# Feature products in quarters of the array and earlier in each block, and a subtraction in four parts, in a recommender kernel

## The reference

```python
e = emb_tables[jnp.arange(F)[None, :], x]             # B=1024, F=32, D=64
gram = jnp.einsum('bid,bjd->bij', e, e)
cross = gram[:, iu, ju]                               # the 496 pairs i < j
h = jnp.concatenate([e.reshape(B, F * D), cross], axis=1)
h = jax.nn.relu(h @ W1 + b1)                          # 2544 -> 1024
h = jax.nn.relu(h @ W2 + b2)                          # 1024 -> 512
y = jax.nn.sigmoid(h @ W3 + b3)                       # 512 -> 1000
```

## Time and profile before

| | |
|---|---|
| median of 3 runs | 507.16 us (505.77 to 508.83) |
| profiled execution | 505.47 us, span 503.7 us |
| TensorE matmul busy | 403.9 us (80%) |
| VectorE, ScalarE busy | 241.4 us (48%), 214.4 us (43%) |
| GpSimd busy | 334.9 us (66%) |
| mean granted TensorE clock | 0.922 of full |
| DMA | 80.15 MB, mean 159 GB/s |

### The profile page before, as it was taken

One profiled execution on the slowest core, in us unless ns is written; L12 is line 12 of the kernel. 1 busy time (PEld: TensorE's weight loads), 2 busy tenths in 40 slices (PEclk: granted clock), 3 DMA queues, 4 the chain that ended last, 5 costly groups with the idle time before them and its releaser, 6 DMA issues.

```text
span 503.7 us, 8367 instructions
## 1 busy us (share of the span) xinstructions
PE 403.9 (80%) x3328; PEld 395.1 (78%) x3328; DVE 241.4 (48%) x326; ACT 214.4 (43%) x358; POOL 334.9 (66%) x517
## 2 busy tenths in 40 slices
PE   0066766767769999878699999968899999897895
PEld 0066766766779999868599999958899999797895
DVE  2233333332348665444348664633586666444650
ACT  3122222223146555543247446442475556434642
POOL 6887888888888878877878778778788880000000
PEclk9997787786979999998889999989799999998998
DMA  7423343321754766623856667618658666167412
GB/s 234 108 62 107 106 105 103 105 65 25 230 189 144 228 188 203 209 64 124 271 191 180 207 197 216 196 23 270 207 164 271 184 181 218 44 216 259 139 51 81
DMA packets 32600, 80.15 MB, mean 159 GB/s; under 512 B 6802, under 2 KB 13106, under 8 KB 32050
## 3 DMA queue, kind: packets, MB, share of 16 engines
q1 hardware_dynamic: 24370, 71.22, 44.8%
q0 software_dynamic: 8192, 8.40, 7.3%
HBM read 69.22 MB, written 10.39 MB: 158 GB/s over the span
## 4 chain that ended last, share of the span: by engine, by line
PE 43%; POOL 33%; issue 10%; DMA 5%; DVE 4%; ACT 2%; SPq 1%; another core or an unknown queue 1%; ACTq 0%; DVEq 0%; POOLq 0%
POOL emb L278 27%; PE h1p L455 8%; PE h1p L456 8%; PE h1p L457 8%; POOL gap L284 6%; PE misc L455 4%; PE misc L485 4%; PE misc L457 4%; PE misc L456 4%; DVE dg L401 3%; DMA gc<-gram_scratch 2%; PE misc L470 2%; ACT dg L315 1%; DMA emb<-tables_dram,idx 1%; DMA gram_scratch<-dg 1%
## 5 line engine op out<-in xcount | busy, mean ns | idle before, releaser
L278 POOL DMA_INDIRECT emb<-tables_dram,idx x256 | 277.0, 1082 | 77.2 <-POOL gap L284 40.6
L385 DVE TENSOR_TENSOR wlo<-wraw,whi 128x1024 fp32r<-128x1024 f32 (+1 forms) x112 | 134.8, 1221 | 63.2 <-ACT whi L301 52.7
L455 PE MATMUL h1p<-xhi,whi 128*128 128x256 f32 x512 | 154.7, 302 | 1.0 <-issue 1.0
L301 ACT CAST whi<-wraw 128x1024 fp32r<-128x1024 f32 (+1 forms) x112 | 117.2, 1049 | 83.8 <-PE h1p L457 56.8
L456 PE MATMUL h1p<-xlo,whi 128*128 128x256 f32 x512 | 151.2, 295 | 0.0
L457 PE MATMUL h1p<-xhi,wlo 128*128 128x256 f32 x512 | 150.9, 295 | 0.0
L455 PEld LDWEIGHTS h1p<-xhi,whi 128*128 128x128 f32 x512 | 105.5, 206 | 1.8 <-issue 1.4
L456 PEld LDWEIGHTS h1p<-xlo,whi 128*128 128x128 f32 x512 | 105.1, 205 | 0.0
L457 PEld LDWEIGHTS h1p<-xhi,wlo 128*128 128x128 f32 x512 | 104.6, 204 | 0.0
L391 DVE TENSOR_TENSOR xlo<-misc,xhi 128x512 fp32r<-128x512 f32 x32 | 22.1, 691 | 101.8 <-ACT z L308 77.6
L470 PE MATMUL misc<-ident,emb 128*128 128x128 f32 x128 | 23.6, 316 | 54.5 <-DMA emb<-tables_dram,idx 54.5
(11 more groups left out here) (34 smaller groups left out, 540.7 us busy)
## 6 DMA issues: line engine op xcount, KB each, us to landing
wraw<-w_dram SPq DMA_DIRECT2D x96, 512.0 KB
wraw<-w_dram SPq DMA_DIRECT2D x16, 500.0 KB
emb<-tables_dram,idx POOLq DMA_INDIRECT x256
gram_scratch<-dg SPq DMA_DIRECT2D x4, 1024.0 KB
out_dram<-res SPq DMA_DIRECT2D x16, 250.0 KB
gram_scratch<-dg SPq DMA_DIRECT2D x4, 512.0 KB
gc<-gram_scratch SPq DMA_DIRECT2D x16, 128.0 KB
xi<-x_dram SPq DMA_DIRECT2D x1, 128.0 KB, 2.1
```

What stands on the lines that cost most here:

```text
L278: nc.gpsimd.indirect_dma_start(emb[:, n % 2, k, t, f * D:(f + 1) * D], None, tables, bass.IndirectOffsetOnAxis(ap=idx[:, BT * n + t, 2 * k ...
L301: nc.scalar.copy(whi[:, u % RING, 0:w], wraw[:, u % RAWS, 0:w]).then_inc(s_whi, 1)
L385: nc.vector.tensor_tensor(wlo[:, u % RING, 0:w], wraw[:, u % RAWS, 0:w], whi[:, u % RING, 0:w].bitcast(fp32), ALU.subtract).then_inc(s_wlo, 1)
L455: nc.tensor.matmul(dst, whi[:, slot, cols], hi, start=start, stop=False, skip_group_check=True)
```

## The change

Four things are changed together.

- The feature products: each 128x128 product of four samples becomes two 64x64 products of two samples. Their operands and results lie on partitions 0 to 63 or 64 to 127, so that each uses one quarter of the array. A group covers 64 samples instead of 32, so there are four groups, and ScalarE and VectorE each copy half of every group (two copies of 512 elements each, instead of four of 256 for every other group).
- The order: the transposes of a block stand earlier, "gram" stands behind emb 7 instead of emb 12 in blocks 1 to 3, and in block 0 behind emb 11. `XRING` holds 16 tiles instead of 8, as the earlier transposes need.
- The subtraction that makes `wlo` is issued in four parts of 256 columns each.
- The waits follow the new number of groups.

In block 0 "gram" stands behind emb 11 and emb 12 follows it, with "tr 7" ahead of emb 11 instead of emb 12. The core of the diff:

```diff
-GROUPS = QB // 8
+GROUPS = QB // 16
-XRING = 8
+XRING = 16
@@ schedule()
-            if n == 0 and k % 2 == 0 and k // 2 + 1 < KP:
-                yield ("tr", n, k // 2 + 1)
-            if n > 0 and k % 2 == 1 and (k + 3) // 2 < KP:
-                yield ("tr", n, (k + 3) // 2)
             yield ("emb", n, k)
...
         if n == 0:
-            yield from emb(n, 0, 13)
+            for m in range(2, KP - 1):
+                yield from emb(n, 2 * m - 4, 2 * m - 2)
+                yield ("tr", n, m)
+            yield from emb(n, 10, 11)
+            yield ("tr", n, KP - 1)
+            yield from emb(n, 11, 12)
         else:
-            yield from emb(n, 0, 2)
             for k in range(4):
+                yield from emb(n, k, k + 1)
+                yield ("tr", n, k + 2)
                 yield from l2(n - 1, k)
-                yield from emb(n, k + 2, k + 3)
-            yield from emb(n, 6, 7)
+            yield from emb(n, 4, 5)
+            yield ("tr", n, 6)
+            yield from emb(n, 5, 6)
+            yield ("tr", n, 7)
             yield from l3(n - 1, 0)
-            yield from emb(n, 7, 9)
             yield from l3(n - 1, 1)
-            yield from emb(n, 9, 13)
+            yield from emb(n, 6, 8)
         yield ("gram", n)
...
@@ gram_diagonal, dg_of
-            return banks.rearrange("p t (q j) -> p j t q", q=4)[:, F * c:F * (c + 1), :, :]
+            return banks.rearrange("p t (q j) -> p j t q", q=8)[:, F * (c % 2):F * (c % 2 + 1), :, :]
...
@@ gram_copies on ScalarE (on VectorE the same, with range(2, 4))
-                for g in range(0, GROUPS, 2):
+                for g in range(GROUPS):
                     act.wait_ge(s_gram, GROUPS * n + g + 1)
-                    for c in range(4):
+                    for c in range(2):
                         last = nc.scalar.copy(dg_of(g, c), gram_diagonal(g, c))
@@ weight_lo
-                nc.vector.tensor_tensor(wlo[:, u % RING, 0:w], wraw[:, u % RAWS, 0:w],
-                                        whi[:, u % RING, 0:w].bitcast(fp32), ALU.subtract).then_inc(s_wlo, 1)
+                for i in range(4):
+                    part = slice(w // 4 * i, w // 4 * (i + 1))
+                    last = nc.vector.tensor_tensor(wlo[:, u % RING, part], wraw[:, u % RAWS, part],
+                                                   whi[:, u % RING, part].bitcast(fp32), ALU.subtract)
+                last.then_inc(s_wlo, 1)
@@ gram on TensorE
-                        pe.wait_ge(s_dgv if g % 2 else s_dga, GROUPS // 2 * n + g // 2)
-                    for q in range(4):
-                        for t in range(BT):
-                            zq = z[D * t:D * (t + 1), 4 * g + q, :, :].rearrange("d c f -> d (c f)")
-                            last = nc.tensor.matmul(misc[:, 2 * (g % 2) + t, P * q:P * (q + 1)], zq, zq,
-                                                    start=True, stop=True)
+                        pe.wait_ge(s_dga, GROUPS * n + g - 1)
+                        pe.wait_ge(s_dgv, GROUPS * n + g - 1)
+                    for q in range(8):
+                        for h in range(2):
+                            for t in range(BT):
+                                zq = z[D * t:D * (t + 1), 8 * g + q, 2 * h:2 * h + 2, :].rearrange("d c f -> d (c f)")
+                                last = nc.tensor.matmul(misc[D * h:D * (h + 1), 2 * (g % 2) + t, D * q:D * (q + 1)],
+                                                        zq, zq, start=True, stop=True)
```

More of the change, by code:

```diff
@@ L50, in schedule @@
     yield ("tr", 0, 0)
+    yield ("tr", 0, 1)
     for n in range(BLOCKS):
         if n == 0:
-            yield from emb(n, 0, 13)
+            for m in range(2, KP - 1):
[4 more added lines that the diff above has]
+            yield from emb(n, 11, 12)
         else:
-            yield from emb(n, 0, 2)
             for k in range(4):
+                yield from emb(n, k, k + 1)
+                yield ("tr", n, k + 2)
                 yield from l2(n - 1, k)
-                yield from emb(n, k + 2, k + 3)
-            yield from emb(n, 6, 7)
+            yield from emb(n, 4, 5)
+            yield ("tr", n, 6)
+            yield from emb(n, 5, 6)
+            yield ("tr", n, 7)
             yield from l3(n - 1, 0)
-            yield from emb(n, 7, 9)
             yield from l3(n - 1, 1)
-            yield from emb(n, 9, 13)
+            yield from emb(n, 6, 8)
         yield ("gram", n)
-        yield from emb(n, 13, 14)
+        if n == 0:
+            yield from emb(n, 12, 13)
+        else:
+            yield from emb(n, 8, 11)
         yield ("move", n)
@@ L68, in schedule @@
             yield from l3(n - 1, 2)
-        yield from emb(n, 14, 15)
+            yield from emb(n, 11, 14)
+        else:
+            yield from emb(n, 13, 14)
         yield ("pairs", n)
-        yield from emb(n, 15, 16)
+        yield from emb(n, 14, 16)
         yield ("pair", n, 0)
@@ L209, in gram_diagonal @@
             banks = misc[F * c:F * (c + 1), 2 * (g % 2):2 * (g % 2) + 2, :]
-            return banks.rearrange("p t (q j) -> p j t q", q=4)[:, F * c:F * (c + 1), :, :]
+            return banks.rearrange("p t (q j) -> p j t q", q=8)[:, F * (c % 2):F * (c % 2 + 1), :, :]
         def dg_of(g, c):
-            return dg[F * c:F * (c + 1), :, :].rearrange("p j (t q) -> p j t q", t=BT)[:, :, :, 4 * g:4 * g + 4]
+            return dg[F * c:F * (c + 1), :, :].rearrange("p j (t q) -> p j t q", t=BT)[:, :, :, 8 * g:8 * g + 8]
         @block.sync
@@ L241, in _ @@
                         sp.wait_ge(s_gc, 64 * n)
-                    sp.wait_ge(s_dga, GROUPS // 2 * (n + 1))
-                    sp.wait_ge(s_dgv, GROUPS // 2 * (n + 1))
+                    sp.wait_ge(s_dga, GROUPS * (n + 1))
+                    sp.wait_ge(s_dgv, GROUPS * (n + 1))
                     sp.dma_start(gd[:, 0:F, :], dg[:]).then_inc(s_gdw, 16)
@@ L397, in gram_copies @@
             def gram_copies(n):
-                for g in range(1, GROUPS, 2):
+                for g in range(GROUPS):
                     dve.wait_ge(s_gram, GROUPS * n + g + 1)
-                    for c in range(4):
+                    for c in range(2, 4):
                         last = nc.vector.tensor_copy(dg_of(g, c), gram_diagonal(g, c))
@@ L465, in transposes @@
                 if n > 0 and m < 2:
-                    pe.wait_ge(s_dga, GROUPS // 2 * n)
-                    pe.wait_ge(s_dgv, GROUPS // 2 * n)
+                    pe.wait_ge(s_dga, GROUPS * n)
+                    pe.wait_ge(s_dgv, GROUPS * n)
                 for k in range(2):
@@ L508, in layer2 @@
                         pe.wait_ge(s_sig, 4 * n)
-                    grams = GROUPS // 2 * (min(n + 1, BLOCKS - 1) if n + 1 < BLOCKS else BLOCKS)
+                    grams = GROUPS * (n + 1)
                     pe.wait_ge(s_dga, grams)
@@ L527, in layer3 @@
                     if n + 1 < BLOCKS:
-                        pe.wait_ge(s_dga, GROUPS // 2 * (n + 2))
-                        pe.wait_ge(s_dgv, GROUPS // 2 * (n + 2))
+                        pe.wait_ge(s_dga, GROUPS * (n + 2))
+                        pe.wait_ge(s_dgv, GROUPS * (n + 2))
                 for c in range(H2 // P):
```

## The result

| | before | changed |
|---|---|---|
| median of 4 runs each | 508.0 us (505.77 to 509.84) | 490.35 us (488.51 to 492.0) |
| span of the profiled execution | 503.7 us | 486.7 us |

The ratio is 0.9641, with a 95% interval of 0.9612 to 0.9669.

A forecast was written before the change was run, and what follows sets the result against it. GpSimd's gathers were taken to bound blocks 1 to 3: last gather, 3 us landing and the work behind give 504.3 + G' - S = 493.8 us of span, 9.9 less, so 497.3 us forecast, range 489 to 512.

The forecast's parts named there:

- G': TensorE's stage of feature products in each block after the change: 9.5 us, against 11.0 in block 3 before.
- S: How much earlier GpSimd's last gather ends through the four-part subtraction: 20 us, bounds 0 and 25.
- landing: Time from the last gather's end on GpSimd until its data has arrived: 3 us, between 1.8 and 4.9.
- the stretch behind tr 7: From block 3's last transposes (tr 7) to the end: 80.2 us before, 85.7 + G' after.
- case 5: The forecast itself, S 14 to 23 and G' 7 to 15: a median of 493 to 504 us; chance 0.62.
- rival 4: Products and freed gathers both at their good ends (G' 6, S 23 or more): median 491 us or under; chance 0.09.
- The bound: GpSimd's gathers, about 99.5 us a block, make the last transposes (tr 7) wait in blocks 1, 2 and 3.
- cool start at tr 7: TensorE's wait for the gather before a block's last transposes cools the array, which costs 1.8 us.
- the factor of the squares: Gathers' held time goes with the sum of squared subtraction durations: factor 0.43, 34.6 us become 14.8.
- VectorE's price: Extra VectorE time for the four-part subtractions: 45 us, from 48% to about 58% busy, nothing taken in the sum.
- The price of the order: Seven TensorE steps, 20.2 us, move behind the last gather, less pair 0's wait (3.7) and cool start (1.8).
- Rival 2: Product quarters cost as much as halves or more: span 499 us at G' 15, 514 at 20; chance of the latter 0.05.

The follow-up runs named there:

- wide_gap: The changed kernel with an iota of 480 columns instead of 96 behind each gather: 571.48 us, ratio 1.1206 to the kernel before.
- no_gap: The changed kernel without the iota and the wait behind each gather: 444.43 us, ratio 0.8727 to the kernel before.
- before_again: The kernel before, unchanged, profiled again on the chip of the third set: 510.56 us over 7 runs.
- after_again: The changed kernel itself, run again on the chip of the second set: 559.84 us, ratio 1.087 to the kernel before.
- old_order_b: The changed kernel with the order of before, quarters and four parts kept, on the second set's chip: 565.74 us, ratio 1.0952 to the kernel before.
- old_order_c: The changed kernel with the order of before, quarters and four parts kept, on a further well supplied chip: 478.47 us, ratio 0.9388 to the kernel before.
- after: The changed kernel as first measured, with all parts of the change against the kernel before: median 490.35 us, ratio 0.9641.

## Why the prediction was right

The sum was 504.3 + G' - S for the span, built from the last gather, its landing and the stretch behind tr 7. The path was right, and the time lies in the range of 489 to 512. But 490.35 us, with a span of 486.7, is below the forecast's own case 5 (493 to 504); it is the time of rival 4 ("both gains at their good ends"), which had a chance of 0.09. Of its two gains one came, G' (5.4, where it had 6); S was 21, near the forecast, and the landing made up the rest.

- *The bound.* Right: GpSimd's clock sets tr 7 in blocks 1, 2 and 3, and the end is the last gather plus the steps behind. Shown by the changed kernel's waits, and by `wide_gap`, whose span moved with the gathers, and `no_gap`, where they ceased to bind. The cool start at tr 7 was put at 1.8 us and is 1.4. That blocks 2 and 3 of the kernel before are set by TensorE is so in its trace, but not in `before_again`. There the same copies stand between the products and a stage takes 11.0 us in every block, so the copies are not what made it 14 to 16; the granted clock is 0.78 and 0.89 in the longer stages of blocks 0 and 2, but 1.00 in the 13.8 us of block 1, and no run shows the rest.
- *Held gathers, S.* 20 forecast, 21.0 measured; the factor of the squares gave 14.8 us of held time from `wlo`, 11.4 was measured. A part costs less than forecast: 1.43 us for four, not 1.6 to 1.7, since 0.085 us and not 0.045 is given back at each join. VectorE's price was mis-sized for the same reason: 24 us for all subtractions instead of 45, and 53% busy instead of 58%, off the path in both. That a gather gets in between two parts held in 61 of 62 cases, and in 444 of 461 in the other traces; I had expected no gather above 1.4 us, and there are two, one behind the unsplit `gclo` and the one that missed the last joins of twelve parts. The rule of the Trainium skill (SBUF — State Buffer, "Who interferes with whom"), that `tensor_tensor` does not stall descriptor generation, does not hold for these indirect gathers.
- *The price of the order.* Seven steps behind the last gather, less the wait and cool start of pair 0: 14.7 us forecast, 14.3 between `after_again` and `old_order_b`, 14.7 between the changed kernel and `old_order_c`. That the order speaks against the change was right, and `old_order_c` shows it in the time, where 9 us are left of it (477.7 against 486.7, on two chips).
- *The mis-sized term: the products, G'.* The forecast was 9.5 us, from 0.035 us a record; it is 5.4 in block 3, from 0.0143. That is the lower bound (0.015), in which the quarters overlap fully. This is 4.1 us of the 7 by which the span was better than forecast. The estimate of 6.4 us from the Trainium skill (TensorEngine Tiling (Array Packing), section "Instruction Overhead") took each of the 256 records for a matmul, and the trace has 3.7 us. But one matmul leaves two records, and the page speaks of matmuls: for 128 of them its 60 cycles give 3.2 us, an estimate from that page which the trace does not contradict.
- *Landing.* 3 us were taken, 1.47 measured in the changed kernel (4.0 in `old_order_c`); this is another 1.5 us, and 1.0 is in S. The prediction had only a range from rows here and no reason for it; that the landing would come out short was luck.
- *Rival 2* (the quarters cost as much as halves) did not come. On two chips a rival that the text did not have came instead: twice as many, shorter instructions in a stage made it 68 us instead of 33 where TensorE's supply is slow. The forecast holds for the chip on which the change was measured, not for these; on the last two chips the changed kernel itself was not run, only variants of it, whose stages of products took 5.3 to 7.3 us.

**Left open.** Why the supply of TensorE is slow beside running gathers in two sets of runs and not in the others, and whether the pace or the presence of gathers sets it. Whether `no_gap` is also the fastest there wasn't tried; nor was the order of before together with `no_gap`. What the split alone or the quarters alone gain where TensorE is well supplied wasn't run. The 0.4% for the split comes from a trace in which TensorE was late in blocks 2 and 3; in `before_again` it waits 14.8 us in all in blocks 1 to 3, and from these waits the split alone should bring some 15 us, or 3%, on that chip (an estimate).

## What to carry to other kernels

When a free-running engine sets the last input, count the work behind that input: steps moved ahead of it are free as long as the engine still comes early to its wait, and steps moved behind it are paid, less only the waits that they fill behind it (20.2 us of steps cost 14.7 here). A long VectorE subtraction with two on-chip inputs held up an indirect gather for its remainder; cutting it in four cost VectorE 17% on that instruction and gave the gathers two thirds of the held time back (34.6 us became 11.4). And measure a change that adds many short TensorE instructions on more than one chip: the same kernel was 3.6% faster in one measurement and 8.7% slower on another chip.

## What the runs showed of the hardware

- On two chips TensorE was slow in a dense stage while GpSimd issued gathers every 1.45 us. In block 0 of `after_again` it did 15 or 16 matmul records in 4 us, in clusters about 0.73 us apart, and in block 2 it was back at 40 in 1.1 us, with the clock at 0.50, 0.6 us after the last gather. On the others the same stage with gathers beside it took 5.3 to 7.5 us. The DMA engines moved 25 GB/s in these stretches, so it is no lack of bandwidth.
- The pace there goes by records and not by columns: 7.5 and 7.8 a us in block 0 for stages of 512 and of 256 records.
- Products of 64x64 on four quarters of the array went at 0.0143 us a record, a quarter of the 0.059 of products of 64x128 on two halves: half the columns, and twice as many at once.
- Subtractions of 256 columns follow each other every 0.34 us, though each is recorded with 0.42.
- The last gather of a block landed 1.4 to 1.5 us after its end where the DMA engines moved 21 to 51 GB/s (`after`), and 4.0 us after it beside weight loads at 272 GB/s (`old_order_c`).
